# An RWKV and mixture-of-experts layer in one kernel: the output projection of time mix in split fp16 and moved behind a shared product, and the prefetch and the zeros of the passage moved

## The reference, cut to what matters

```python
# x: (4096, 256); every layer norm takes mean and variance over the 256 channels
xn = layer_norm(LN(x), g1, b1)
k, v = mix(xn, mk) @ Wk.T, mix(xn, mv) @ Wv.T        # mix: a weighted sum with the token before
sr   = sigmoid(mix(xn, mr) @ Wr.T)
rwkv = sr * wkv(time_decay, time_first, k, v)        # a scan over the tokens
x2   = LN(x) + rwkv @ Wo.T                           # the output projection
xn2  = layer_norm(x2, g2, b2)
kf   = relu(mix(xn2, fk) @ Wk_ffn.T) ** 2            # 1024 wide
x3   = x2 + sigmoid(mix(xn2, fr) @ Wr_ffn.T) * (kf @ Wv_ffn.T)
x1   = x + LN(x3)
xf   = LN(x1)
e    = argmax(xf @ Wg)                               # one of 8 experts per token
y    = geglu(xf; w1s, w2s, w3s) + geglu(xf; W1[e], W2[e], W3[e])
out  = x1 + LN(y)
```

## Time and profile before

| | us |
|---|---|
| median of 3 runs | 1005.57 (1005.17 to 1005.67) |
| the profiled execution, its own time | 1008.09 |
| its span | 1006.1 |
| TensorE busy | 930.5 (92%) |
| VectorE busy | 721.6 (72%) |
| ScalarE busy | 585.8 (58%) |
| GpSimd busy | 588.9 (59%) |
| mean granted TensorE clock | 0.972 of full speed |

### The profile page before, as it was taken

How to read it: one execution, slowest core, us unless ns; L and a number is a source line. 1 busy time by engine, 2 the same in 40 slices (tenths; PEclk the granted TensorE clock), 3 DMA queues, 4 the chain that set the end, 5 groups by cost and what they waited for, 6 DMA issues and landing times.

```text
span 1006.1 us, 27987 instructions
## 1 busy us (share of the span) xinstructions
PE 930.5 (92%) x9734; PEld 840.3 (84%) x9734; DVE 721.6 (72%) x1651; ACT 585.8 (58%) x1014; POOL 588.9 (59%) x800
## 2 busy tenths in 40 slices
PE   2377999999999999999999999779999999999994
PEld 2266888888888888888888878679999999999994
DVE  6888999999999999999999985524444444444442
ACT  4486777878878868868868755223333333333330
POOL 5446667767867866866866542434454555555553
PEclk9697999999999999999999999889999999999998
DMA  7112252351352252153162253935787778576510
GB/s 239 64 54 75 84 178 66 115 198 48 115 211 66 80 209 82 64 209 104 43 224 81 86 209 121 322 139 171 246 273 232 236 264 272 159 260 209 164 56 21
DMA packets 82089, 152.09 MB, mean 151 GB/s; under 512 B 5421, under 2 KB 62894, under 8 KB 76912
## 3 DMA queue, kind: packets, MB, share of 16 engines
q1 hardware_dynamic: 35104, 73.99, 21.5%
q10 hardware_dynamic: 42368, 60.38, 18.7%
q0 software_dynamic: 4560, 16.98, 4.4%
HBM read 183.59 MB, written 46.25 MB: 228 GB/s over the span
## 4 chain that ended last, share of the span: by engine, by line
PE 70%; DVE 8%; POOL 7%; issue 6%; ACT 3%; DMA 2%; ACTq 1%; SPq 1%; POOLq 0%; DVEq 0%
PE up L365 14%; PE up L367 14%; PE up L366 14%; PE yp L365 6%; PE yp L367 6%; PE yp L366 6%; PE yp L571 2%; PE yp L574 2%; PE yp L587 2%; PE tp L374 2%; DVE arena L1004 1%; POOL mix_s L1579 1%; DVE er L1105 1%; POOL routed_rows L1612 1%; POOL sh_s L1573 1%
## 5 line engine op out<-in xcount | busy, mean ns | idle before, releaser
L365 PE MATMUL up<-mix_s,arena 128*128 128x128 f16 x1248 | 213.4, 220 | 0.0
L366 PE MATMUL up<-mix_s,arena 128*128 128x128 f16 x1248 | 213.3, 220 | 0.0
L367 PE MATMUL up<-mix_s,arena 128*128 128x128 f16 x1248 | 213.3, 220 | 0.0
L365 PE MATMUL up<-xf_s,arena 128*128 128x256 f16 x512 | 140.6, 275 | 1.9 <-issue 1.9
L1678 POOL TENSOR_TENSOR kf_s<-ex,kf_s 128x512 f16<-128x512 f32 x78 | 90.1, 1156 | 87.9 <-ACT kf_s L964 87.8
L367 PE MATMUL up<-xf_s,arena 128*128 128x256 f16 x512 | 140.7, 275 | 0.0
L366 PE MATMUL up<-xf_s,arena 128*128 128x256 f16 x512 | 140.7, 275 | 0.0
L1445 DVE SCALAR_TENSOR_TENSOR ex<-up,ex 128x512 f32<-128x512 f32 x78 | 54.0, 692 | 105.8 <-ACT ex L958 105.6
L365 PEld LDWEIGHTS up<-mix_s,arena 128*128 128x128 f16 x1248 | 123.0, 99 | 1.0 <-DVE ex L1445 0.8
L366 PEld LDWEIGHTS up<-mix_s,arena 128*128 128x128 f16 x1248 | 123.0, 99 | 0.4
L367 PEld LDWEIGHTS up<-mix_s,arena 128*128 128x128 f16 x1248 | 123.0, 99 | 0.0
(11 more groups left out here) (226 smaller groups left out, 2910.0 us busy)
## 6 DMA issues: line engine op xcount, KB each, us to landing
arena<-w_split ACTq DMA_DIRECT2D x113, 1024.0 KB
arena<-in_W SPq DMA_DIRECT2D x24, 1024.0 KB, 6.9
w_split<-arena SPq DMA_DIRECT2D x24, 1024.0 KB, 9.5
rows<-routed_rows ACTq DMA_DIRECT2D x39, 261.0 KB, 2.9
arena<-w_split SPq DMA_DIRECT2D x9, 1024.0 KB
normed<-routed_rows ACTq DMA_DIRECT2D x37, 128.0 KB, 2.5
x_in<-in_x SPq DMA_DIRECT2D x16, 256.0 KB, 2.8
x_res<-in_x SPq DMA_DIRECT2D x16, 256.0 KB, 2.8
```

The source lines that it names most:

```text
L365: pe.matmul(out, stat(0), mov(0), start=first, stop=False)
L366: pe.matmul(out, stat(0), mov(1), start=False, stop=False)
L367: return pe.matmul(out, stat(1), mov(0), start=False, stop=last)
```

## The change

Three things change. First, the output projection: `oT` joins the weights that are split (`small["o"]`, as piece 3 of the own weights). ScalarE's `rw_hi` rounds rw to fp16 into `rw_s` and VectorE's `rw_lo` takes the rest; `output()` becomes a `token_major` of 12 fp16 matmuls, and `value()`, which writes val again, waits for `rw_lo` instead of `output()`. The split weight carries a factor 64, which the value copy takes out (scale 1/64). Second, the place: `output()` stands behind `shared_up(2)` instead of before it. Third, the passage: `likely_slots` waits for the scatter of chunk 13; SP writes four of the eight blocks of zeros and ScalarE the other four, two by two between its gelus of step 17; and in step 17 the fourth gelu stands before the third `sh_hi`.

```diff
--- before.py
+++ after.py
@@ -64,8 +64,7 @@
         routed_rows = nc.dram_tensor("routed_rows", (E * REGION, ROW), F32).ap()
 
 
-        small = {n: sb("w_" + n, [2, CT, C], F16) for n in ("k", "v", "r", "fr")}
-        w_o = sb("w_o", [CT, C])
+        small = {n: sb("w_" + n, [2, CT, C], F16) for n in ("k", "v", "r", "o", "fr")}
         w_fk = sb("w_fk", [2, CT, F], F16)
         w_fv = sb("w_fv", [FT, C])
         w_gate = sb("w_gate", [2, CT, E], F16)
@@ -115,6 +114,7 @@
         state = sb("state", [3, CT, CH + 1])
         top, aa, bb = (state[:, n] for n in range(3))
         dist = sb("dist", chan)
+        rw_s = sb("rw_s", [2] + chan, F16)
         den, now = mixed[0:2]
         ex = sb("ex", [4, CT, CH])
         x2 = sb("x2", tok)
@@ -185,19 +185,19 @@
             return w[:, :, :, :].rearrange("p h k n -> p h (k n)")
 
         pieces = [(tiles(a[n]), CT, C, flat(small[w]))
-                  for n, w in (("kT", "k"), ("vT", "v"), ("rT", "r"), ("frT", "fr"))]
+                  for n, w in (("kT", "k"), ("vT", "v"), ("rT", "r"), ("oT", "o"), ("frT", "fr"))]
         pieces.append((tiles(a["gate"]), CT, E, flat(w_gate)))
         pieces.append((tiles(a["fkT"]), CT, F, flat(w_fk)))
         for m, n in enumerate(("w1s", "w2s", "w3s")):
             pieces.append((tiles(a[n]), (CT, CT, FT)[m], (F, F, C)[m], shared_w[:, m]))
         N_OWN = len(pieces)
-        NEEDS_KVR, NEEDS_FFN, NEEDS_SHARED = 3, 6, 8
-
-        OWN_HI = {(-2, 0): (0, 3), (-1, 2): (3, 4), (0, 0): (4, 6), (0, 2): (6, 7), (1, 1): (7, 9)}
-        OWN_LO = {(-2, 0): (0, 3), (-1, 1): (3, 4), (0, 1): (4, 6), (1, 3): (6, 7), (2, 3): (7, 8), (2, 0): (8, 9)}
-        OWN_LOADS = {(-1, 0): (4, 6), (0, 0): (6, 7), (0, 1): (8, 9), (1, 1): (7, 8)}
-
-        OWN_BUFFER = [0, 1, 2, 4, 0, 1, 3, 1, 4]
+        NEEDS_KVR, NEEDS_ATT, NEEDS_FFN, NEEDS_SHARED = 3, 4, 7, 9
+
+        OWN_HI = {(-2, 0): (0, 3), (-1, 2): (3, 5), (0, 0): (5, 7), (0, 2): (7, 8), (1, 1): (8, 10)}
+        OWN_LO = {(-2, 0): (0, 3), (-1, 1): (3, 5), (0, 1): (5, 7), (1, 3): (7, 8), (2, 3): (8, 9), (2, 0): (9, 10)}
+        OWN_LOADS = {(-1, 0): (5, 7), (0, 0): (7, 8), (0, 1): (9, 10), (1, 1): (8, 9)}
+
+        OWN_BUFFER = [0, 1, 2, 3, 4, 0, 1, 3, 1, 4]
         own_raw = raw + [c.rearrange("p h n -> p (h n)").bitcast(F32) for c in cut]
 
         def own_pieces(when, i, part=0):
@@ -286,17 +286,15 @@
                 sp.dma_start(w_split[bass.ds(e, 1), :, m], cut[m % 2]).then_inc(S(f"expert_out{m}"), 16)
 
             sp.dma_start(x_in[:], x_tok[0]).then_inc(S("x_in"), 16)
-            for n in range(3):
+            for n in range(5):
                 load_own(n)
-            sp.dma_start(w_o[:], tiles(a["oT"])).then_inc(S("o_in"), 16)
-            load_own(3)
             sp.dma_start(w_fv[:], tiles(a["fvT"])).then_inc(S("fv_in"), 16)
 
             def zeros_at_ends():
 
                 sp.wait_ge(S("end_at"), 1)
                 sp.wait_ge(S("zero_row"), 1)
-                for e in range(E):
+                for e in range(E // 2):
                     at = sp.value_load(end_at[0:1, e:e + 1], min_val=0, max_val=E * REGION - P)
                     sp.dma_start(routed_rows[bass.ds(at, P)], zero_row).then_inc(S("zeroed"), 16)
 
@@ -308,6 +306,7 @@
 
             def likely_slots():
 
+                sp.wait_ge(S("scattered1"), 16 * TT * (NC // 2 - 1))
                 for m in range(3):
                     sp.wait_ge(S(f"expert_lo{m}"), E)
                     sp.wait_ge(S(f"expert_out{m}"), 16 * (E - 1))
@@ -579,14 +578,10 @@
                     if not on(c0):
                         return
                     if at_step(i, 0):
-                        pe.wait_ge(S("o_in"), 16)
-                    wait(pe, S("rw"), c0 + 1)
+                        pe.wait_ge(S("piece_lo"), NEEDS_ATT)
+                    wait(pe, S("rw_lo"), c0 + 1)
                     wait(pe, S("sig"), c0)
-                    for t in range(TT):
-                        for k in range(CT):
-                            m = pe.matmul(yp[0][:, t, :], val[:, k, t * P:(t + 1) * P], w_o[:, k, :], start=(k == 0),
-                                          stop=(k == CT - 1))
-                    m.then_inc(S("wo_mm"), 1)
+                    token_major(yp[0], rw_s, lambda s, k: small["o"][:, s, k, :], CT, "wo_mm")
 
                 def shared_down(c, q):
                     if not on(c):
@@ -642,8 +637,8 @@
                 for q in range(4):
                     channel_mix_down(q)
                 shared_gate(2)
+                shared_up(2)
                 output()
-                shared_up(2)
                 shared_gate(3)
                 shared_up(3)
                 if at_step(i, NC) or at_step(i, NC + 1):
@@ -724,9 +719,9 @@
 
                 def value():
                     if on(c0):
-                        wait(act, S("wo_mm"), c0)
+                        wait(act, S("rw_lo"), c0)
                         wait(act, S("v_mm"), c0 + 1)
-                        act.activation(val[:], up[1][:], ACT.Copy).then_inc(S("val"), 1)
+                        act.activation(val[:], up[1][:], ACT.Copy, scale=1 / WS).then_inc(S("val"), 1)
 
                 def receptance():
                     if on(c0):
@@ -809,6 +804,12 @@
                         act.activation(sh_s[:, 0, 2 * g:2 * g + 2, :], gu[g % GUS][:],
                                        ACT.Copy).then_inc(S("sh_hi"), 1)
 
+                def rw_hi():
+                    if on(c0):
+                        wait(act, S("rw"), c0 + 1)
+                        wait(act, S("wo_mm"), c0)
+                        act.activation(rw_s[:, 0], val[:], ACT.Copy).then_inc(S("rw_hi"), 1)
+
                 def mix_hi(m):
                     if on(i + 1):
                         wait(act, S("mix"), CT * (3 * (i + 1) + m + 1))
@@ -829,6 +830,13 @@
                 def own(part):
                     for n in own_pieces(OWN_HI, i, part):
                         own_hi(n)
+
+                def zeros_at_end(e):
+                    if at_step(i, NC + 1):
+                        act.wait_ge(S("end_at"), 1)
+                        act.wait_ge(S("zero_row"), 1)
+                        at = act.value_load(end_at[0:1, e:e + 1], min_val=0, max_val=E * REGION - P)
+                        act.dma_start(routed_rows[bass.ds(at, P)], zero_row).then_inc(S("zeroed"), 16)
 
                 def late_hi():
                     for e, m in late_piece(i, p, h):
@@ -868,6 +876,8 @@
                 gelu(0)
                 if at_step(i, NC):
                     late_hi()
+                zeros_at_end(E // 2)
+                zeros_at_end(E // 2 + 1)
                 gelu(1)
                 if not at_step(i, -1):
                     ln0(i + 1, 1 - p)
@@ -887,12 +897,17 @@
                     early_hi()
                 mix_hi(0)
                 sh_hi(0)
+                zeros_at_end(E // 2 + 2)
+                zeros_at_end(E // 2 + 3)
                 if at_step(i, NC + 1):
                     gelu(2)
                 mix_hi(1)
                 sh_hi(1)
+                if at_step(i, NC + 1):
+                    gelu(3)
                 if not at_step(i, NC):
                     late_hi()
+                    rw_hi()
                     early_hi()
                 mix_hi(2)
                 own(2)
@@ -900,7 +915,8 @@
                     gelu(2)
                 if last:
                     sh_hi(2)
-                gelu(3)
+                if not at_step(i, NC + 1):
+                    gelu(3)
                 exp_table()
                 if not last:
                     sh_hi(2)
@@ -1118,6 +1134,10 @@
                 wait(dve, S("denominator"), 4 * c + 4)
                 wait(dve, S("num"), c + 1)
                 dve.tensor_tensor(val[:], val[:], er[:], ALU.mult).then_inc(S("rw"), 1)
+
+            def rw_lo(c):
+                wait(dve, S("rw_hi"), c + 1)
+                dve.tensor_tensor(rw_s[:, 1], val[:], rw_s[:, 0], ALU.subtract).then_inc(S("rw_lo"), 1)
 
             def x2_sum(c, b):
                 wait(dve, S("wo_mm"), c + 1)
@@ -1321,6 +1341,8 @@
                 if on(i + 1):
                     mix0(i + 1, 1 - p, 2)
                     carry(i + 1)
+                if on(c0):
+                    rw_lo(c0)
                 if on(c1):
                     x3_gate(c1)
                     x3_sum(c1)
```

## The result

| | before | after |
|---|---|---|
| median, us | 1005.62 (1005.17 to 1006.72, 4 runs) | 1050.07 (1049.02 to 1052.36, 4 runs) |
| ratio | | 1.0448, 95% interval 1.0433 to 1.0463 |
| span of the profiled execution | 1006.1 | 1047.2 |

The account below looks back on a forecast made before the run. TensorE was taken to bound the chunk loop, with the chain to normed2's transposes almost level. Chunk loop +11.9 and passage -3.4 gave +8.5, 1016.6 for the profiled execution, 1014 for the median; range 1004 to 1019.

Parts of the forecast that it names:

- Part 1, the products: Output projection: 12 fp16 products replace four fp32 ones, 1.31 us instead of 1.73, saving TensorE 0.42 a step.
- Part 2, the place: Projection behind shared_up(2): TensorE waits about 1.2 us at every transposes of normed2; an even step gets +0.74.
- the named step: Transposes of normed2, 6.2 us behind x2, expected to hold TensorE with waits of about 1.2 a step.
- Part 3, the cut of rw: Before the projection: 0.24 us uncovered in odd steps, making them +0.72; VectorE's extra 0.7 a step stays hidden.
- Part 4, the passage: From chunk loop to slots: scatter of chunk 13 lands 4.8 us earlier, slots start 3.4 earlier, so -3.4.
- VectorE becomes the bound: Rival: with 0.7 us more a step, VectorE's order in the loop costs another 0.6 a step, +7, 1021; chance 0.06.
- The new waits lower the clock: Rival: waits in the chunk loop lower TensorE's clock, some 5 us lost 13 times, 1079; chance 0.03.

Follow-up runs that it names:

- e10: Changed kernel with the projection back before shared_up(2) and x3_sum reading one operand from PSUM; 1010.35 us, ratio 1.0041 to the kernel before.
- e14: e10 with num ahead of the halo copy, reciprocal and rw ahead of the mixes, rw_lo behind the first, rw_hi before mix_hi(0); 1053.18 us, ratio 1.0490.
- e2: Kernel before with only output() moved behind shared_up(2), fp32 product kept, no cut of rw; 1016.38 us, ratio 1.0104.
- e11: e7 with VectorE's shared(2) put ahead of x2_sum; 1028.06 us, ratio 1.0222 to the kernel before.
- e1: Kernel before with one more VectorE subtraction per step, of rw_lo's shape and at its place, result unread; 1037.62 us, ratio 1.0313.
- e7: Changed kernel, same order, with x3_gate writing to PSUM so x3_sum has one SBUF operand, shared_down waiting for x3_sum; 1013.84 us, ratio 1.0086.
- e4: Kernel before with the passage's three edits alone (prefetch's wait, zeros shared with ScalarE, fourth gelu earlier); 1006.19 us, ratio 0.9999.
- e16: Kernel before with only the zeros shared with ScalarE and the fourth gelu of step 17 earlier; one execution, 1004.22 us.
- e3: Changed kernel with output() back before shared_up(2), all else kept; 1037.59 us, ratio 1.0322 to the kernel before.
- e5: Changed kernel with x3_gate and x3_sum ahead of rw_lo on VectorE, operands in SBUF; 1048.52 us, ratio 1.0432 to the kernel before.
- e12: Kernel before with 24 short VectorE and GpSimd measurements ahead of it, started together; VectorE's two-SBUF-operand instruction, coming first, kept 0.69 us.
- e13: Short measurements ahead of the kernel before, VectorE's two-SBUF-operand instruction coming second, beside GpSimd additions or near an indirect DMA; 1.31 us beside one addition.
- e6: Changed kernel with GpSimd's inverse2 ahead of sh_lo(1) and mix_lo(2); 1048.47 us, ratio 1.0420 to the kernel before.

## Why the prediction was wrong, point by point

- **Part 1, the products: held.** Twelve starts of 0.109 from 596.94 to 598.25 are the 1.31 of the sum. They come only with the cut of rw, and neither e10 nor e14 found a place for it where the 0.42 was left over.
- **Part 2, the place: size near, wait misnamed.** I had 0.74 a step with the products at the transposes. e2 lost 11.4 in 13 steps, 0.88 with the old products, where my terms give 1.16, and the wait is at projection k for `shared(2)`, 3.41 behind x2. I had followed one chain behind x2_sum, `normed2`, and not the bank that the moved `shared_up(2)` hands on. That both chains end within 0.1 (346.52 against 346.58 in e2), so that the place costs about what was forecast, is luck. The earlier trace rows was also misread: of its 22.9 only 1.6 lie in the loop from 130 to 600. And e11, which puts `shared(2)` first, shows the named step (the transposes) binding next, though with x2 itself 0.70 late.
- **Part 3, the cut of rw: this is the step that failed.** "VectorE also gets 0.7 a step, hidden behind its wait for the projection (1.11 in the earlier trace rows)". It was priced at its own time, which was right (0.68), and at nothing as a shift of what follows. e1 has such an instruction alone: +32.6. It moves `x3_sum` by 0.60 against GpSimd, onto the start of an addition, and lengthens it from 0.69 to 3.18 on average. e7, with the shift and without the hold, measures 1013.84, next to the 1014 of the sum. That is in part luck: +9.1 with no gain in the passage, where the sum had +11.9 and -3.4, so two errors of some 3 cancel. The trace of before had the warning: `val<-mixed,dist` (L1115) takes 1.32 on average in the loop, all twelve beside GpSimd's `delta`: nine took 1.53, and in three it took 0.68 and `delta` 1.93 to 2.01 instead of 1.4. The prediction has no row of it.
- **Part 4, the passage: the scatter right, the gain 0.9 for 3.4** in e4's trace and none in the timed runs. The mis-sized term is the rate behind the scatter, 333 GB/s for 365, as above. The rule cited there (DMAs of several engines share the 16 DMA engines) agrees: in e4 SP issues its four blocks in 4.7 instead of eight in 9.2, and the last block lands no earlier; with the zeros alone (e16) it lands 0.3 earlier.
- **The rivals.** "VectorE becomes the bound" had 0.06 and a price of 0.6 a step; VectorE's order did cost, but by a hold that nothing in the rival names, and 2.5 + 0.7 a step. "The new waits lower the clock" had 0.03. It came as an addition: in the step from 313 TensorE stood 3.09 and then had a granted clock of 0.72 for 6 us (2.4 GHz, then 1.2, matmul starts 0.21 apart), and from x2 to the transposes it was 7.71 (316.51 to 324.22); in the one above it stood 2.26, kept 1.00, and it was 6.15. At the old place, where it stood at most 2.1 (e3), the loop's clock is 1.00 (in e5, with waits up to 3.7, 0.98), and the hold costs 27.2 (e3 less e10) instead of 36.2; the 3% of 430 us, some 13, would cover the 9 between. That the clock is the whole of these 9 was not tested.
- **The chances.** Slower 0.75 was right; the range ended 31 us short, since its bound for the added instruction came from rows of that instruction's kind alone and none asked what the instructions behind it would meet.

## What to carry to other kernels

An instruction added to an in-order engine moves all behind it; before it is called hidden, lay what follows over the other engines' timeline at its new time. On VectorE look for instructions with two SBUF operands that come to stand where a GpSimd addition begins, and read the spread of a group (0.68 to 1.53 us in L1115), not its mean. With one operand in PSUM such an instruction was not held here (e7, e12); reordering mostly handed the hold to the next.

## What the runs showed of the hardware

- A VectorE instruction with two SBUF operands (0.69 alone) took 1.31 behind one GpSimd addition and 3.58 when it began 0.47 us into the issue of an indirect DMA that two additions followed (e13); 0.69 at the same place in the issue with no addition behind it (e6), and 0.69 beside the same additions with one operand in PSUM (e7).
- Of such instructions that began during the issue of an indirect DMA, the 52 with GpSimd's next work 0.11 to 0.54 us behind their start were held, the 57 with it 0.71 us or more behind were not (traces of sixteen kernels).
- The held side's record starts at its usual time and only grows; the profile shows busy time, no wait. GpSimd is held too when VectorE's instruction comes first: an addition 1.70 for 1.26, one of 128x2 0.64, where such a one takes 0.20 in the earlier trace rows (e12), and the issue of an indirect DMA 1.39 for 0.98 (e13) and 1.40 for 0.97 (kernel before).
